# Weighted values of the second attention on eight 64x32 tiles with operands swapped and turned back, scores by units, and banks dealt anew

## The reference

```
f, g, hv = x @ wf + bf, x @ wg + bg, x @ wh + bh
o = softmax(g @ f.T) @ hv @ wo + bo
y = relu(norm(concat([gamma * o + x, x]) @ wc + bc))
```

```
q = (y @ w_q + b_q).reshape(B * 8, 256, 16)
k, v = (pool(y) @ w_k + b_k).reshape(B * 8, 64, 16), (same with w_v, b_v)
out = softmax(q @ k.T / 4) @ v
result = out.reshape(B, 16, 16, 128) @ w_o + b_o + y
```

## Time and profile before

| what | us |
|---|---|
| median of 3 runs | 51.65 (51.53 to 52.11) |
| the profiled execution | 51.91 |
| its span, first to last instruction | 50.1 |
| PE busy | 43.7 |
| DVE busy | 31.5 |
| ACT busy | 25.0 |
| POOL busy | 17.7 |

### The profile page before, as it was taken

One profiled execution on the slowest core, in us unless ns is written; L12 is line 12 of the kernel. 1 busy time (PEld: TensorE's weight loads), 2 busy tenths in 40 slices (PEclk: granted clock), 3 DMA queues, 4 the chain that ended last, 5 costly groups with the idle time before them and its releaser, 6 DMA issues.

```text
span 50.1 us, 875 instructions
## 1 busy us (share of the span) xinstructions
PE 43.7 (87%) x306; PEld 35.2 (70%) x306; DVE 31.5 (63%) x76; ACT 25.0 (50%) x58; POOL 17.7 (35%) x39
## 2 busy tenths in 40 slices
PE   1999969999999999999999999799994998699600
PEld 1997649988938988676967867597572994698300
DVE  1003693460964169998559997879992499837720
ACT  4703077675997540579970857705547024940000
POOL 5949300000074995352007492930049600000000
PEclk9999999999999999999999999999999999999995
DMA  0499700000000000000000000000000200023022
GB/s 0 130 273 281 302 37 3 0 0 0 0 0 0 0 0 13 0 0 0 0 0 0 7 0 0 0 13 0 0 0 7 98 0 0 0 105 108 3 52 52
DMA packets 1556, 1.86 MB, mean 37 GB/s; under 512 B 656, under 2 KB 1168, under 8 KB 1552
## 3 DMA queue, kind: packets, MB, share of 16 engines
q1 hardware_dynamic: 1552, 1.81, 11.6%
HBM read 1.29 MB, written 0.52 MB: 36 GB/s over the span
## 4 chain that ended last, share of the span: by engine, by line
PE 56%; DVE 19%; DMA 11%; POOL 4%; issue 2%; SPq 2%
DMA x_rest<-in_x_rest 11%; PE bk_y L353 7%; PE quad L397 6%; PE bk_y L374 6%; DVE d L676 6%; PE bk_x L418 5%; DVE max L675 5%; PE quad L405 4%; PE bk_y L349 3%; PE bk_a L326 3%; PE bk_x L368 3%; PE quad L292 3%; PE quad L313 3%; POOL q_heads L233 2%; PE bk_a L340 2%
## 5 line engine op out<-in xcount | busy, mean ns | idle before, releaser
L554 ACT ACTIVATE p<-d 128x512 f32<-128x512 f32 x8 | 5.0, 630 | 8.6 <-DVE d L676 8.6
L418 PEld LDWEIGHTS bk_x<-v_heads,pt 128*128 128x128 f32 x56 | 6.8, 191 | 0.8 <-issue 0.5
L418 PE MATMUL bk_x<-v_heads,pt 128*128 128x102 f32 x56 | 7.2, 276 | 0.0
L226 POOL TENSOR_TENSOR p0n<-p,rsum 128x512 f32<-128x512 f32 x3 | 3.1, 1039 | 11.4 <-DVE rsum L649 11.4
L675 DVE TENSOR_REDUCE max<-quad 128x8 f32<-128x512 f32 x8 | 5.4, 674 | 2.1 <-PE quad L397 2.1
L676 DVE TENSOR_TENSOR d<-quad,max 128x512 f32<-128x512 f32 x8 | 5.5, 691 | 0.3
L559 ACT COPY pt<-quad 128x512 f32<-128x512 f32 x8 | 4.6, 579 | 1.3 <-PE quad L405 1.2
L405 PE MATMUL quad<-prep,p 128*128 128x128 f32 x32 | 5.0, 279 | 0.0
L656 DVE TENSOR_REDUCE xp_sum<-y 128x56 f32<-128x504 f32 x4 | 2.7, 667 | 3.2 <-ACT y L545 3.2
L405 PEld LDWEIGHTS quad<-prep,p 128*128 128x128 f32 x32 | 3.6, 140 | 1.5 <-ACT p L554 1.1
L281 PE MATMUL quad<-warm 128*128 128x128 f32 x16 | 3.7, 390 | 1.1 <-DVE warm L719 1.1
(11 more groups left out here) (109 smaller groups left out, 84.3 us busy)
## 6 DMA issues: line engine op xcount, KB each, us to landing
late<-in_late SPq DMA_DIRECT2D x1, 427.5 KB, 5.9
x_rest<-in_x_rest SPq DMA_DIRECT2D x1, 384.0 KB, 5.3
out_t<-res SPq DMA_DIRECT2D x3, 128.0 KB, 1.8
prep<-in_prep SPq DMA_DIRECT2D x1, 291.5 KB, 2.8
first<-in_first SPq DMA_DIRECT2D x1, 153.5 KB, 2.3
out_t<-res SPq DMA_DIRECT2D x2, 64.0 KB, 1.7
```

Of the source, the lines that this page charges most:

```text
L226: v.tensor_tensor(p0n[:, b], p0[:, b], rsum0[:, b].unsqueeze(2).to_broadcast([P, T, N]), ALU.mult).then_inc(p0_kept, 1)
L418: last = mm(to.rearrange("n (r w) -> n r w", r=WIDE), pt1[:, b, u, j, s, :], v_heads[:, b, h, :].unsqueeze(1).to_broadcast([P, WIDE, VW]), ...
L554: sc.activation(p1[:, b, u].rearrange("n j s m -> n (j s m)"), d1[:, b, u].rearrange("n j h m -> n (j h m)"), ACT.Exp, scale=1.0 / TEMP).t ...
```

## The change

1. `attend_1` swaps its operands and goes onto tiles: `v_heads` (64 rows of contraction, 32 columns: 16 values and 16 of ones) is the weight, the turned probabilities (64 rows x 128 columns) are streamed. A unit is eight products on 2 row tiles x 4 column tiles, and its output has values on partitions, in two banks: `pair` (the old `bk_a` and `bk_b`), for the last image in `quad`. ACT's new `keep_ot1` copies it out, and PE's new `turn_back` (two transposes a unit) puts queries back on partitions in `bk_x`. `p1` and `pt1` are laid out by `e` (the two channel groups of a 32-row block), with both halves of the image in one transpose.
2. Values need no spreading by a mask: POOL adds the bias only, and `turn_values` is one transpose, copied by ACT as 128 columns. `v_heads` is cleared to one in one instruction.
3. `scores_1` is called per unit (four products and one increment), waits only for the same unit of the image before, and DVE starts a unit when its own scores are there.
4. Banks: `conv_0` writes `bk_x` for images 1 and 2, `queries(3)` writes `bk_y`, `conv_1` writes `bk_y`; no queries wait for `o_kept` now, while `turn_values(b)` does, for the image before.
5. The result of images 0 to 2 leaves DVE: ACT's `keep_res` adds the bias, POOL's new `result` adds `y`.
6. The lists are written in another order: the two middle fills go to the start, `weights_1` goes ahead of `project_fg(0)`, all stage-one work comes before image 1's scores, and queries and pooling of images 2 and 3 come there too. `pool_1` runs on DVE for all four images, in both kernels.

```diff
-VW = E * D + E
-WIDE = 3
...
+        v_heads = sb("v_heads", B, J, E, VW)
         max1 = sb("max1", B, UNITS, JU, HALF * E)
         d1 = sb("d1", B, UNITS, JU, HALF * E, M)
-        p1 = sb("p1", B, UNITS, JU, HALF, E * M)
-        pt1 = sb("pt1", B, UNITS, JU, HALF, P)
+        p1 = sb("p1", B, UNITS, JU, E, HALF * M)
+        pt1 = sb("pt1", B, UNITS, JU, E, P)
+        ot1 = sb("ot1", B, UNITS, HALF, P)
...
+        pair, bk_x, bk_y = bank("pair", 2), bank("bk_x"), bank("bk_y")
+        bk_a, bk_b = pair[:, 0], pair[:, 1]
...
+        y_bank = [bk_y[:, 0:N], bk_x[:, 0:N], bk_x[:, 0:N], bk_y[:, 0:N]]
+        q_bank = [bk_x[:, 0:N], bk_x[:, 0:N], bk_x[:, 0:N], bk_y[:, 0:N]]
...
+        def ot1_bank(b, u):
+            return pair[:, :, u * P:(u + 1) * P] if b < LAST else quad[:, u * JU:(u + 1) * JU, N:N + P]
...
+            def result(b):
+                pool.wait_ge(proj_kept, b + 1)
+                v.tensor_tensor(res[:, b, :], proj[:, b, :], y[:, b, 0:H, :].rearrange("c h w -> c (h w)"),
+                                ALU.add).then_inc(res_kept, 1)
...
+            result(0)
+            result(1)
+            result(2)
...
+                elif b < LAST:
+                    pe.wait_ge(q_turned, b)
                 else:
-                    pe.wait_ge(kv_turned, b)
-                mm(bk_y[:, 0:N], wsum[:], image(b), start=True, stop=False)
+                    pe.wait_ge(kv_turned, 2)
+                mm(y_bank[b], wsum[:], image(b), start=True, stop=False)
...
                 pe.wait_ge(pooled, b + 1)
-                pe.wait_ge(y_kept, b + 1)
+                if b == 2:
+                    pe.wait_ge(q_turned, B)
+                elif b:
+                    pe.wait_ge(kv_turned, b)
                 mm(bk_y[:], xp[:, b].rearrange("c j q -> c (j q)"), l_("wkv"), start=True, stop=True).then_inc(kv_ps, 1)
...
             def turn_values(b):
-                pe.wait_ge(v_masked, b + 1)
-                if b < LAST:
-                    pe.wait_ge(q_turned, b + 2)
+                pe.wait_ge(v_biased, b + 1)
+                if b == 0:
+                    pe.wait_ge(q_turned, 3)
                 else:
-                    pe.wait_ge(o_kept, LAST)
-                for s in range(HALF):
-                    last = turn(bk_x[:, s * P:(s + 1) * P], v_wide[:, b, s].rearrange("c e k p -> c (e k p)"), ident)
-                last.then_inc(v_ps, 1)
-
-            def scores_1(b):
-                pe.wait_ge(q_kept, b + 1)
-                pe.wait_ge(k_kept, b + 1)
-                if b == 0:
+                    pe.wait_ge(o_kept, b)
+                turn(bk_x[:, 0:P], v_rows[:, b].rearrange("c s k p -> c (s k p)"), ident).then_inc(v_ps, 1)
+
+            def scores_1(b, u):
+                if u == 0:
+                    pe.wait_ge(q_kept, b + 1)
+                    pe.wait_ge(k_kept, b + 1)
+                if b:
+                    pe.wait_ge(pt1_kept, UNITS * (b - 1) + u + 1)
+                elif u == 0:
                     pe.wait_ge(v0_kept, B)
                     wait_fg(LAST)
-                else:
-                    pe.wait_ge(pt1_kept, UNITS * b)
                 for s in range(HALF):
-                    for j in range(J):
+                    for j in range(u * JU, (u + 1) * JU):
                         r = slice(j * Q, (j + 1) * Q)
-                        last = mm(quad[:, j, s * P:(s + 1) * P], q_heads[r, b, s].rearrange("c i p -> c (i p)"),
-                                  k_heads[r, b, s].rearrange("c e k p -> c (e k p)"), start=True, stop=True)
-                        last.then_inc(s1_ps, 1)
+                        to = quad[:, j, 0:N].rearrange("n (e s m) -> n e s m", e=E, s=HALF)[:, :, s, :]
+                        last = mm(to, q_heads[r, b, s].rearrange("c i p -> c (i p)"),
+                                  k_heads[r, b, s].rearrange("c e k p -> c e (k p)"), start=True, stop=True)
+                last.then_inc(s1_ps, 1)
 
             def turn_1(b, u):
                 pe.wait_ge(exp1_done, UNITS * b + u + 1)
                 for j in range(JU):
-                    for s in range(HALF):
-                        last = turn(quad[:, u * JU + j, N + s * P:N + (s + 1) * P], p1[:, b, u, j, s, :], ident)
+                    for e in range(E):
+                        last = turn(quad[:, u * JU + j, N + e * P:N + (e + 1) * P], p1[:, b, u, j, e, :], ident)
                 last.then_inc(pt1_ps, 1)
 
             def attend_1(b, u):
                 pe.wait_ge(v_kept, b + 1)
                 pe.wait_ge(pt1_kept, UNITS * b + u + 1)
-                if (b, u) == (LAST, 1):
-                    pe.wait_ge(kv_turned, B)
+                if (b, u) == (0, 0):
+                    pe.wait_ge(pt0_kept, count0(LAST))
+                elif b < LAST:
+                    pe.wait_ge(ot1_kept, UNITS * b + u)
                 for s in range(HALF):
                     for j in range(JU):
-                        h = s * J + u * JU + j
-                        at = (u * HALF + s) * JU + j if b < LAST else s * JU + j
-                        to = (bk_x if b < LAST else o_last[u])[:, at * VW:(at + WIDE) * VW]
-                        last = mm(to.rearrange("n (r w) -> n r w", r=WIDE), pt1[:, b, u, j, s, :],
-                                  v_heads[:, b, h, :].unsqueeze(1).to_broadcast([P, WIDE, VW]), start=True, stop=True)
+                        for e in range(E):
+                            rows, at = slice(s * M, (s + 1) * M), slice((j * E + e) * VW, (j * E + e + 1) * VW)
+                            last = mm(ot1_bank(b, u)[at, s, :], v_heads[rows, b, u * JU + j, e, :],
+                                      pt1[rows, b, u, j, e, :], start=True, stop=True)
+                last.then_inc(ot1_ps, 1)
+
+            def turn_back(b, u):
+                pe.wait_ge(ot1_kept, UNITS * b + u + 1)
+                if u == 0:
+                    pe.wait_ge(v_kept, b + 1)
+                elif b == LAST:
+                    pe.wait_ge(proj_kept, LAST)
+                for s in range(HALF):
+                    at = u * HALF + s if b < LAST else s
+                    last = turn((bk_x if b < LAST else o_last[u])[:, at * P:(at + 1) * P], ot1[:, b, u, s, :], ident)
                 if b == LAST or u == UNITS - 1:
                     last.then_inc(o_ps, 1)
 
             def conv_1(b):
...
             fill(WARM)
+            fill(1)
+            fill(1)
+            weights_1()
             project_fg(0)
             fill(1)
-            weights_1()
...
+            turn_1(0, 0)
+            conv_0(3)
+            queries(2)
+            turn_1(0, 1)
+            queries(3)
             turn_values(0)
...
+            def keep_ot1(b, u):
+                act.wait_ge(ot1_ps, UNITS * b + u + 1)
+                sc.copy(ot1[:, b, u], ot1_bank(b, u)).then_inc(ot1_kept, 1)
+
+            def keep_res(b):
+                act.wait_ge(res_ps, b + 1)
+                sc.activation(proj[:, b, :], bk_y[:, 0:N], ACT.Identity, bias=l_("bo1")).then_inc(proj_kept, 1)
...
-                dve.wait_ge(s1_ps, HEADS * (b + 1))
+                dve.wait_ge(s1_ps, UNITS * b + u + 1)
```

More of the change, by code:

```diff
@@ L51 @@
 BLK = G
-VW = E * D + E
-WIDE = 3
+VW = Q
 UNITS = 2
@@ L142, in build @@
         quad = bank("quad", 4)
-        bk_a, bk_b, bk_x, bk_y = bank("bk_a"), bank("bk_b"), bank("bk_x"), bank("bk_y")
+        pair, bk_x, bk_y = bank("pair", 2), bank("bk_x"), bank("bk_y")
+        bk_a, bk_b = pair[:, 0], pair[:, 1]
         wow_at, w3_at, c_at = slice(0, C), slice(C, 2 * C), slice(2 * C, 2 * C + 1)
@@ L217, in setup @@
                 pool.wait_ge(xp_clear, 1)
-                for e in range(E):
-                    rows = slice(64 * e, 64 * e + 64)
-                    for c in range(E):
-                        v.memset(v_heads[rows, :, :, E * D + c:E * D + c + 1], 1.0 if c == e else 0.0).then_inc(v_ones, 1)
-                pool.wait_ge(v_ones, E * E)
+                v.memset(v_heads[:], 1.0).then_inc(v_ones, 1)
             def norm_0(b):
@@ L262, in _ @@
             values(0)
+            keys(0)
             bias_q(1)
+            norm_0(3)
+            values(1)
             keys(1)
-            norm_0(3)
+            bias_q(2)
+            bias_q(3)
             keys(2)
-            values(1)
-            bias_q(2)
             values(2)
+            values(3)
             keys(3)
-            bias_q(3)
-            values(3)
+            result(0)
+            result(1)
+            result(2)
         @block.tensor
@@ L367, in queries @@
                     pixels = y[:, b, s * H // 2:(s + 1) * H // 2, :].rearrange("c h w -> c (h w)")
-                    last = mm(bk_x[:, s * P:(s + 1) * P], pixels, l_("wq"), start=True, stop=True)
+                    last = mm(q_bank[b][:, s * P:(s + 1) * P], pixels, l_("wq"), start=True, stop=True)
                 last.then_inc(q_ps, 1)
@@ L549, in keep_v @@
                 act.wait_ge(v_ps, b + 1)
```

(20 more changed lines are left out.)

190 lines of the change are left out of this document (97 added, 93 removed).

## The result

The changed kernel took 50.0 us in the median of four runs (49.55 to 50.24) against 51.7 us; the ratio is 0.965, 95% interval 0.956 to 0.974. Run again beside the first experiments its ratio was 0.9575 (0.951 to 0.964). The profiled execution took 50.24 us, its span is 48.4 us, 1.7 us less than before; forecast were 49.95 us and -1.7 us. Medians and ranges are of all runs of a kernel; a ratio leaves out those that took over 1.5% more than its fastest run.

The account below looks back on a forecast made before the run. PE's work was taken to bound the kernel up to about 30 us, then a ring. Stretch terms 0, -1.4, -1.85, +1.35 and +0.2 sum to -1.7 us: 51.65 to 49.95 us, range 49.0 to 51.7.

Parts of the forecast that it names:

- What bounds the kernel: PE's summed work sets the time up to about 30 us; after that a loop of dependent steps across engines does.
- a ring: From about 30 us: queries, VectorE's block transpose, POOL's bias, scores, VectorE's maximum and subtraction set the time.
- The new unit: Weighted values of one unit, 16 passes on eight 64x32 tiles: 0.63 us, four at a time, 0.24 less than before.
- rival 2: Weighted values with all eight tiles at once: 0.41 us a unit, kernel 49.2 us; chance 0.13.
- Rival 1: Tiles of one row group do not overlap: 1.06 us a unit, kernel 52.6 us; chance 0.12.
- Scores by units: Second-stage scores, eight passes per unit: 0.41 to 0.44 us where a unit stands alone, taken as 0.44.
- First stretch: From 7.00 us to image 0's scores: changes sum to 0, stays 11.66 us; first softmax's 0.7 us slip hidden.
- Second stretch: Image 0's scores to image 2's: work -0.36, waits -1.05, together -1.4 us, from 13.38 to 11.98.
- Third: Image 2's scores to image 3's: work 4.0 plus new waits 0.8 makes 4.8 us, -1.85 from 6.66.
- Fourth: Image 3's scores to the last eviction: 10.7 us, +1.35 from 9.34, with ScalarE's copies in the way.
- Landing: Output's landing after the last eviction: +0.2 us, 2.06 to 2.26; DMAs issued 0.5 apart, evictions end 0.3 apart.
- rival 5: Short bursts let the clock fall to 1.2 GHz in the last 15 us: +2 to +4 us, 52 to 54; chance 0.04.

Follow-up runs that it names:

- image3_late: Changed kernel with image 3's second stage put back late, behind image 1's output: 54.25 us median of four; its one run at mean clock 0.99 took 52.9.

## Why the prediction was right, step by step

**What bounds the kernel: right.** PE's sum of work up to 30 us, then a ring. Doubling the tile passes showed that about three quarters of what is added to PE's work is paid (1.3 of 1.7 us in the profile).

**The new unit: mis-sized.** Forecast 0.63 us, four passes at a time; measured 0.38, eight at a time, with 0.17 fixed. The size is rival 2's, the lower bound; the fixed 0.2 us of a burst held (0.17). Over eight units that is 2.0 us less work on PE than forecast. With turning back (0.22) the forecast unit cost 0.85 us against 0.87 before, so by the prediction's own sum the tiles gained nothing; measured they cost 0.60 and gained 0.27 a unit. Rival 1, tiles of one row group one after the other, is out: eight passes were in work in one slice, and the doubled burst shows eight at a time, which takes all four column tiles of both row groups. The page "TensorE: Matmul & The Clock Gate" of the Trainium skill, section on packing small matmuls, says that loads overlap running matmuls only where the row group differs, and in the same section that loads into a background weight buffer are pulled ahead as well. The first rule does not bind these column tiles: the 16 loads of a unit, 104 ns each, took 0.18 us together, most of it under running passes; whether the background buffer is the reason no row here shows. The page "TensorEngine Tiling (Array Packing)" of the Trainium skill, section Key Properties, says that a switch of tiling mode drains TensorE. The trace agrees: at thirteen of the fifteen switches behind a pass of 128 columns between 19 and 39 us (full array to small tiles, back, and between 32x128 and 64x32) the next pass starts 0.20 us later, where 0.11 is streaming; the other two took 0.25, and 0.57 with a wait for ScalarE. So about 0.09 us of the fixed 0.17 stands at the burst's end, and another 0.09 us in front of it, which is in no unit cost of the prediction. The neighbours take longer too: keys and values between two bursts 1.06 us for 0.86, the value turn behind a burst 0.26 for 0.11. The count was off by one besides: four bursts became fourteen, not thirteen.

**Scores by units: mis-sized the other way.** Forecast 0.44 us, measured 0.64. The burst before had four row tiles at work because its inner loop went over four groups `j`, each on its own 32 rows. A unit has only two of them, so it runs two passes at a time: 8 / 2 x 0.107 + 0.2 = 0.63. The diff shows that; I carried the "four at a time" over without counting the tiles of a unit. For images 2 and 3 that is 4 x 0.2 = 0.8 us, and image 1's two units took 0.86 where 0.66 was forecast. Alone a unit pays its fixed part by itself; image 1's two stand next to each other on different row tiles, the second starts 0.21 us after the first, and 0.86 us is all they take. The slower scores (about 1.0 us of work) and the late start (0.7 us) are the terms that stand against rival 2's 49.2 us, which did not come although its unit did.

**First stretch: wrong by 0.7 us.** I held the slip of the first softmax to be hidden behind three projections. It wasn't: PE reached them at 7.94 to 8.16 us in the two profiles of this kernel, as its queue had first products at half pace in front, while the load had landed before. The term put at nothing was the dependence on the clock: over eight profiles the same start gives 18.68 to 19.39 us for image 0's scores, by when the clock rises. The old start gave back 0.5 us in the first pair of traces. The landing at 7.0 us, which the prediction took as fixed, was at 5.6 to 6.4 us in nine of the eleven profiles.

**Second stretch: right (12.00 for 11.98), by errors that cancel**: two units 0.5 less, scores of image 1 0.2 more, and the rest in pieces that take longer than priced, such as the 1.06 us of keys and values; PE has no wait there at all. **Third: 4.57 for 4.8**, the units 0.5 less, the scores 0.4 to 0.5 more, and PE idle for 0.3 us where 0.8 of new waits were forecast; image 3's scores stood at 35.91 for 35.4. **Fourth: 10.18 for 10.7**; ScalarE's queue is in the chain as forecast, 1.27 us in a row. **Landing: right** (2.31 for 2.26).

So the sum was right to 0.1 us with three terms wrong: -2.0, about +1.0 and +0.7, and the rest in the waits. That they cancel is luck. What the working had wrong in kind is the share-out: it gave the early start of image 3 most of the gain (-1.4 and -1.85) and the tiles none. By it the kernel without tiles would have taken about 50 us; it took 52.35. Without the tiles all the rest together is worth nothing (1.0045), and with them a late image 3 costs 2.9 us (one run). What the tiles are worth in the order of before, with nothing else changed, was not run and stays open; `image3_late` comes nearest, but starts image 3 later than the kernel before did.

**The clock (rival 5): not in this kernel, but near.** From the first record to the last slice it stayed at full speed; two variants with a thin stretch of PE work had it fall, at a cost of 1.0 to 2.0 us in one. Where it did cost this kernel time was at the start, which the rival did not name.

## What to carry to other kernels

Count, for each burst of small products, how many different tiles of the array it has, not how many products. Here passes streamed as many at a time as there were tiles (two, four and eight), a burst alone paid 0.17 to 0.2 us on top and about 0.09 on the work in front of it, so splitting one along the loop that walks over the tiles cost its parallelism as well. One engine's queue was the bound here, and moving an image's work earlier, together with the other changes, did not pay until the work itself got shorter: it came back in the last stretch. Work put ahead of the first landing can run while the clock is still low, so its price is not the one read in the middle of the trace. And a sum that comes out right is no proof of its terms: cut the trace of after at the same places and compare them one by one.

## What the runs showed that was not expected

- Eight products of 64x32 with 128 float32 columns, 16 passes, take 0.38 us on PE's path where four full-array products of 102 columns take 0.87; their weight loads take 0.18 us together.
- In two variants a thin stretch of PE (a wait of 1.76 us in one, several short ones that made 1.0 of 4 us in the other) was followed by a granted clock of 0.50 over 2 us and of 0.62 over 4 us; the order of the second with more tile work ran at 1.00, and was still slower, by the work.
- At the start PE ran at half pace until 4.1 us in one execution and until 6.7 in another, with the same fills from 1.05 us on; the profile's 1.00 there stands for a missing record.
- A switch between the full array and small tiles, either way, or between two shapes of small tiles put 0.20 us between the starts of two passes where streaming puts 0.11 (thirteen of fifteen in one trace).
